# Layer 3 attention: how the mixed bank is turned, summed over its halves and divided

## The chip, the cores and the metric

The kernel runs on one core of a Trainium2 chip. The metric is device time in microseconds (us) of one launch, which computes a whole four-layer decoder. The engines are TensorE (PE, with its weight loads as PEld), VectorE (DVE), ScalarE (ACT), GpSimd (POOL) and the DMA queues. They run side by side and meet at semaphores.

## The reference

Each of the four layers has self-attention, cross-attention and a feed-forward part; `x` is 16 x 128 x 256, 2048 tokens of 256 features. The change touches only the attention of layer 3, which lets all 2048 tokens attend to each other, in 16 heads of 16 features:

```python
proj = jnp.einsum('bsd,ed->bse', x, proj_w) + proj_b
flat = jnp.transpose(proj.reshape(B, S, H, hd), (2, 0, 1, 3)).reshape(H, B * S, hd)
q = jnp.einsum('hnd,hde->hne', flat, wq)
k = jnp.einsum('hnd,hde->hne', flat, wk)
logits = jnp.einsum('hne,hme->hnm', q, k) / jnp.sqrt(jnp.asarray(D, x.dtype))
attn = jax.nn.softmax(logits, axis=-1)
out = jnp.einsum('hnm,hmd->hnd', attn, flat)
```

`out` is put back into token order and added to `x`.

## The kernel before

The kernel is a row of phases. In a phase every engine has its own program, written out in a fixed order, and waits on semaphores by count; a phase ends when all its engines have ended. The phase here is called "heads" (`l3_attn`, second half). It takes the 16 heads as 8 pairs and the 2048 queries as 4 chunks of 512, which makes 32 units `u` of 32 steps `n`. A step handles one tile of 128 keys of one of the pair's two heads (`a`).

All engines count the same steps:

- PE, `probe` (L4821): computes logits the other way round (queries on partitions), 48 steps ahead, only to find each query's maximum. They go through four banks of PSUM, two for each pair of steps.
- DVE, `peak_of` (L4874): the maximum over two such banks. After a unit's 16 of these, `peak_of_all` (L4880) reduces once more, and POOL and DVE (`part`, `turn_rows`, `lay_rows`) put the maximum into two extra rows of the queries.
- PE, `score` (L4811): keys on partitions, 512 queries along the row, less the maximum. Three banks (`SB`) take turns. ACT, `exp` (L4911), reads the bank and writes `attn`.
- PE, `mix` (L4836): values times `attn`, some eight steps behind. A bank holds four strips of 32 partitions: two heads times two halves of the key tiles. Row 16 of a strip is the softmax's sum, since the values carry a column of ones (`VW` is 17 of `PAD` 32).

When a unit's mixing is done, its end is worked off in the following unit, at fixed steps:

- step 6: ACT copies the mixed bank to `output` in SBUF (`out`, L4922). The next `mix` waits for it.
- step 15: PE turns `output` with four 128 x 128 transposes (`unturn`, L4846) into the next of the three score banks; the slot counts as one of the "score" jobs.
- step 15: ACT copies the whole turned bank to `unturned` (`take`, L4928), which frees the bank: `slot_free` waits on the common counter `read`, which `exp` and `take` raise.
- step 17: POOL adds the two halves (`add_halves`, L4984) to `sums`.
- step 24: DVE takes the reciprocal of the softmax's sums (L4891); POOL multiplies (L4990) and adds the product to `x` (L4994).

Between steps 14 and 16 PE has no probe and score to run beside each other until the turning is over: score 15 stands in front of it, and the probes of step 16 behind it.

Of the kernel before, what the change touches and what calls it, by code (L numbers as in the profile page):

```python
# [13 lines left out]
ALU = mybir.AluOpType  # L14
ACT = mybir.ActivationFunctionType
# [17 lines left out]
def sl(i, n=P):  # L33
    return slice(i * n, (i + 1) * n)
# [4479 lines left out]
def l3_attn(k):  # L4514
# [23 lines left out]
    with ExitStack() as stack:  # L4538
# [185 lines left out]
        peak = sb(k, stack, "peak", [P, 2, 4, 2])  # L4724
        peak_parts, peak_rows = (sb(k, stack, m, [P, 2, 4, 2, PAD]) for m in ("peak_parts", "peak_rows"))
        output = sb(k, stack, "output", [P, CHUNK])
        unturned = sb(k, stack, "unturned", [P, 4, 4, PAD])
        sums, fresh = sb(k, stack, "sums", [P, 4, 2, VW]), sb(k, stack, "fresh", [P, 4, 2, D])
        share = sb(k, stack, "share", [P, 4, 2])
        mixed_bank = k.ps[:, 7, :]  # L4730
        steps = range(-LEAD, TOTAL + SPAN)
        OUT, UNTURN, SUM, DIVIDE, TURN, RAISE = 6, 15, 17, 24, 5, 8

        def scored(n):
            return 0 <= n < TOTAL
# [10 lines left out]
        for n_ in steps:  # L4746
# [3 lines left out]
            for job in jobs:  # L4750
                slot_of[job] = len(slot_of)

        def bank(job):
            return k.ps[:, slot_of[job] % SB, :]

        names = ("loaded0 loaded1 pool_step cleared fetched probed maxed peaked parted rows_turned raised scored read mixed outed "
                 "unturned summed shared added value_made value_took biased")
        with phase(k, "heads", names) as (block, s):
            loaded = [s[f"loaded{i}"] for i in range(2)]

# [25 lines left out]
            @block.tensor  # L4786
            def _(pe):
                def slot_free(job):
                    if slot_of[job] >= SB:
                        pe.wait_ge(s["read"], slot_of[job] - SB + 1)  # L4790
                    else:
                        pe.wait_ge(s["value_took"], QT // 2)

                def value(t):
                    i, o = t // 2, t % 2
                    if i >= SB and o == 0:
                        pe.wait_ge(s["value_took"], i - SB + 1)
                    for kt in range(KD):
                        last = nc.tensor.matmul(k.ps[:, i % SB, sl(o, DIM)], xT[t // GROUP][:, kt, sl(t % GROUP)], wp[:, kt, :],
                                                start=kt == 0, stop=kt == KD - 1)  # L4800
                    if o:
                        last.then_inc(s["value_made"], 1)

                def score(n):
                    u, i = n // SPAN, n % SPAN
                    pair, c, kt, a = u // CHUNKS, u % CHUNKS, i // 2, i % 2
                    rows = slice(TILE * a, TILE * a + DEEP)
                    if i == 0:
                        pe.wait_ge(s["raised"], 8 * (u + 1))
                    slot_free(("score", n))  # L4810
                    nc.tensor.matmul(bank(("score", n)), keys[pair % 2][rows, sl(kt)], queries[pair % 2][rows, sl(c, CHUNK)],  # L4811
                                     start=True, stop=True).then_inc(s["scored"], 1)

                def probe(p):
                    pair, t, c, a = p // (CHUNKS * SPAN), p // 8 % QT, p // 2 % 4, p % 2
                    rows = slice(TILE * a, TILE * a + DEEP)
                    if p % (CHUNKS * SPAN) == 0:
                        pair_landed(pe, pair)
                    if p >= PB and p % 2 == 0:
                        pe.wait_ge(s["maxed"], (p - PB) // 2 + 1)  # L4820
                    last = nc.tensor.matmul(k.ps[:, SB + p % PB, :], queries[pair % 2][rows, sl(t)], keys[pair % 2][rows, sl(c, CHUNK)],  # L4821
                                            start=True, stop=True)
                    if p % 2:
                        last.then_inc(s["probed"], 1)

                def mix(m, half):
                    u, part = m // 8, m % 8
                    columns = sl(half, CHUNK // 2)
                    if half == 0:
                        pe.wait_ge(s["read"], slot_of["score", 4 * m + 3] + 1)  # L4830
                    if part == 0 and half == 0:
                        pe.wait_ge(s["fetched"], u // CHUNKS + 1)
                        if u >= 1:
                            pe.wait_ge(s["outed"], u)
                    for strip in range(4):
                        last = nc.tensor.matmul(mixed_bank[sl(strip, PAD), columns], head_values[:, u // CHUNKS % 2, strip % 2, 2 * part + strip // 2, :],  # L4836
                                                attn[:, (4 * m + strip) % RING, columns], start=part == 0 and half == 0, stop=part == 7 and half == 1,
                                                skip_group_check=True)
                    if half == 1:
                        last.then_inc(s["mixed"], 1)  # L4840

                def unturn(u):
                    pe.wait_ge(s["outed"], u + 1)
                    slot_free(("unturn", u))
                    for b in range(4):
                        last = nc.tensor.transpose(bank(("unturn", u))[:, sl(b)], output[:, sl(b)], k.ident[:, :])  # L4846
                    last.then_inc(s["unturned"], 1)

                for n in steps:
                    if n % 2 == 0:  # L4850
                        for p in (n + LEAD, n + LEAD + 1):
                            if p < TOTAL:
                                probe(p)
                        if 0 <= (n + LEAD) // 2 - 1 < QT:
                            value((n + LEAD) // 2 - 1)
                        if scored(n):
                            score(n)
                        if scored(4 * (n // 4 - 2)):
                            mix(n // 4 - 2, n % 4 // 2)
                        if scored(n + 1):  # L4860
                            score(n + 1)
                    if ended_at(n, UNTURN) is not None:
                        unturn(ended_at(n, UNTURN))

            @block.vector
            def _(dve):
# [20 lines left out]
                                peak_parts[:, r % 2, :, :, :].rearrange("p b a c -> p (b a c)")).then_inc(s["rows_turned"], 1)  # L4887

                def divide(u):
                    dve.wait_ge(s["summed"], u + 1)  # L4890
                    v.reciprocal(share[:, :, :].unsqueeze(3), sums[:, :, :, D:VW]).then_inc(s["shared"], 1)  # L4891

                for n in steps:
                    p = n + LEAD
                    if p < TOTAL:
# [10 lines left out]
            def _(act):  # L4906
# [11 lines left out]
                def out(u):  # L4918
                    act.wait_ge(s["mixed"], 8 * (u + 1))
                    if u >= 1:  # L4920
                        act.wait_ge(s["unturned"], u)
                    nc.scalar.activation(output[:, :], mixed_bank, ACT.Copy).then_inc(s["outed"], 1)  # L4922

                def take(u):
                    act.wait_ge(s["unturned"], u + 1)
                    if u >= 1:
                        act.wait_ge(s["summed"], u)
                    nc.scalar.activation(unturned[:, :, :, :].rearrange("p b a w -> p (b a w)"), bank(("unturn", u)),  # L4928
                                         ACT.Copy).then_inc(s["read"], 1)

                for i in range(QT // 2):
                    take_values(i)
                for n in steps:
                    if scored(n):
                        exp(n)
                    if ended_at(n, OUT) is not None:
                        out(ended_at(n, OUT))
                    if ended_at(n, UNTURN) is not None:
                        take(ended_at(n, UNTURN))

            @block.gpsimd
            def _(pool):
# [43 lines left out]

                def add(u):
                    pair, c = u // CHUNKS, u % CHUNKS
                    pool.wait_ge(s["shared"], u + 1)
                    g_.tensor_tensor(fresh[:, :, :, :], sums[:, :, :, 0:D], share[:, :, :].unsqueeze(3).broadcast_to([P, 4, 2, D]),  # L4990
                                     ALU.mult).then_inc(s["added"], 1)
                    pool.wait_ge(s["added"], 2 * u + 1)
                    x = k.x[:, sl(c, 4), sl(pair, 2 * D)].rearrange("p b (a d) -> p b a d", a=2)
                    g_.tensor_tensor(x, x, fresh[:, :, :, :], ALU.add).then_inc(s["added"], 1)  # L4994
                    done["added"] += 2

                def add_bias(i):
                    pool.wait_ge(s["value_took"], i + 1)
# [8 lines left out]
                for n in steps:  # L5007
# [8 lines left out]
                        lay_rows(row_at(n, RAISE))  # L5016
                    if n > 0 and n % (CHUNKS * SPAN) == CHUNKS * SPAN - 16 and n // (CHUNKS * SPAN) + 1 < PAIRS:
                        fetch(n // (CHUNKS * SPAN) + 1)
                    if ended_at(n, SUM) is not None:
                        add_halves(ended_at(n, SUM))  # L5020
                    if ended_at(n, DIVIDE) is not None:
                        add(ended_at(n, DIVIDE))


def lay_out_rest(i, w):
# [224 lines left out]
```

## Time and profile before

| | |
|---|---|
| Time, median of 3 runs | 3270.43 us (3260.84 to 3272.57) |
| The profiled execution's own time | 3283.28 us |
| Its span | 3281.5 us |
| Granted TensorE clock, mean over the span | 0.951 |
| The phase "heads" | about 2300 to 3030 us of the span |
| Units in it | 32 |

A row of the timeline merges instructions of one kind that follow each other: its count is behind the x, and its length reaches from the first one's start to the last one's end. An f32 matmul appears as two records (and two weight loads); a transpose and an fp32r matmul (probe, score) as one. Matmuls are pipelined and their ends are modelled, so the starts are what a reader should compare.

### The profile page before, as it was taken

The page shows a single profiled execution, that of the slowest core. Times are in us where ns is not written, and L with a number is a line of the kernel's source. Part 1 is how long each engine was busy: PE and PEld are TensorE (multiplying, and loading weights), DVE is VectorE, ACT ScalarE, POOL GpSimd, SP SyncE. Part 2 cuts the span into 40 slices and gives each one's busy share as a digit, 9 for nine tenths or more (in the row PEclk, how much of TensorE's full clock was granted, in tenths as well). Part 3 has the DMA queues.
Part 4 walks back from the last instruction along what each step waited for, and adds up shares of the span by engine and source line. Part 5 has one row for each costly group of instructions (what it writes and reads, how often), then busy time and mean ns, then how long its engine had stood idle before and what let it go on. Part 6 is the DMA issues. An engine that isn't in the chain of part 4 may idle for free. (4 is left out here: it accounts for less than half of the span.)

```text
span 3281.5 us, 59482 instructions
## 1 busy us (share of the span) xinstructions
PE 2987.2 (91%) x20953; PEld 1853.7 (56%) x20957; DVE 2145.8 (65%) x4263; ACT 1900.2 (58%) x4408; POOL 1131.2 (34%) x1285
## 2 busy tenths in 40 slices
PE   7979889999988899988799989898899999999989
PEld 4656568888755466634577656454333333333667
DVE  6767663233586566676677557425699999995672
ACT  7958725555443344445666635212388888888554
POOL 4535555442450122223366643101222211211333
PEclk9989879999999999999899999899699999999989
DMA  9400056676640000031000051223311111100300
GB/s 310 138 10 1 1 231 201 211 216 182 189 128 2 26 1 1 1 131 62 5 1 1 1 193 53 91 87 119 77 21 21 21 21 21 21 2 20 124 1 26
DMA packets 158996, 243.69 MB, mean 74 GB/s; under 512 B 21450, under 2 KB 130666, under 8 KB 153434
## 3 DMA queue, kind: packets, MB, share of 16 engines
q1 hardware_dynamic: 144690, 201.93, 19.9%
q0 software_dynamic: 13824, 37.77, 3.6%
q8 instruction: 173, 2.83, 0.4%
q14 instruction: 117, 0.96, 0.1%
q10 hardware_dynamic: 192, 0.20, 0.0%
HBM read 131.14 MB, written 107.12 MB: 73 GB/s over the span
## 5 line engine op out<-in xcount | busy, mean ns | idle before, releaser
L4874 DVE TENSOR_REDUCE peaks<-ps 128x2 f32<-128x1024 f32 x512 | 619.0, 1220 | 63.1 <-PE ps L4821 61.2
L4911 ACT ACTIVATE attn<-ps 128x512 f32<-128x512 f32 x1024 | 558.9, 596 | 99.4 <-PE ps L4811 42.2
L4821 PE MATMUL ps<-keys,queries 50*128 50x512 f32 x1024 | 367.6, 463 | 19.0 <-DMA queries<-parts 15.4
L4811 PE MATMUL ps<-queries,keys 50*128 50x512 f32 x1024 | 383.4, 454 | 0.0
L4836 PE MATMUL ps<-attn,head_values 128*32 128x256 f32 x4096 | 331.8, 396 | 9.2 <-ACT output L4922 9.2
L4811 PEld LDWEIGHTS ps<-queries,keys 50*128 50x128 f32 x1024 | 157.3, 188 | 215.2 <-ACT attn L4911 197.1
L1239 POOL TENSOR_TENSOR attn_w<-attn_w,attn_share 128x512 f32<-128x512 f32 x128 | 131.7, 1050 | 373.8 <-DVE attn_share L1085 373.8
L2163 PE MATMUL ps<-experts,tileT 128*128 x884 | 227.9, 379 | 2.0 <-ACT tileT L2242 2.0
L2413 DVE COPY hiddenT<-ps 128x128 f32<-128x128 f32 x237 | 69.0, 291 | 245.1 <-PE ps L2170 242.7
L4836 PEld LDWEIGHTS ps<-attn,head_values 128*32 128x32 f32 x4096 | 82.3, 108 | 197.7 <-issue 108.1
L4821 PEld LDWEIGHTS ps<-keys,queries 50*128 50x128 f32 x1024 | 146.4, 189 | 34.1 <-issue 26.1
L2163 PEld LDWEIGHTS ps<-experts,tileT 128*128 128x128 f32 x884 | 150.7, 190 | 17.2 <-issue 2.3
L2248 ACT ACTIVATE gate<-ps 128x128 f32<-128x128 f32 x237 | 65.8, 278 | 161.3 <-PE ps L2163 159.2
L2183 PE MATMUL ps<-experts,hiddenT 128*128 (+1 forms) x474 | 144.6, 387 | 7.3 <-issue 3.5
L1076 DVE TENSOR_REDUCE attn_peak<-ps 128x4 f32<-128x512 f32 x128 | 87.6, 685 | 95.5 <-PE ps L958 95.5
L4961 POOL CAST peak_parts<-peak 128x8 fp32r<-128x8 f32 x32 | 6.3, 197 | 399.8 <-DVE peak L4880 381.1
L2075 POOL DMA_INDIRECT rows<-expert_rows,index x96 | 94.0, 979 | 110.9 <-ACT normed L2259 71.6
L972 PE MATMUL ps<-xT,L_xattn_Wq 128*128 128x512 f32 x256 | 124.7, 610 | 7.7 <-ACT qT L1176 6.2
L2062 POOL DMA_INDIRECT routed_rows<-rows,index x96 | 96.8, 1009 | 83.5 <-ACT normed L2259 47.8
L4976 POOL CAST queries<-peak_rows 2x128 fp32r<-2x128 f32 x256 | 73.5, 287 | 123.5 <-DVE peak_rows L4886 109.8
L4334 POOL TENSOR_TENSOR lasting<-lasting,pairs 128x512 f32<-128x512 f32 x64 | 81.0, 1279 | 85.3 <-ACT lasting L4259 85.3
L1187 ACT ACTIVATE attn_wT<-ps 128x512 f32<-128x512 f32 x128 | 70.5, 594 | 67.5 <-PE ps L989 67.5
(732 smaller groups left out, 7189.8 us busy)
## 6 DMA issues: line engine op xcount, KB each, us to landing
tile_in<-routed_rows SPq DMA_DIRECT2D x244, 128.0 KB, 2.3
expert_rows<-normed SPq DMA_DIRECT2D x136, 128.0 KB, 1.9
routed_rows<-zeros SPq DMA_DIRECT2D x2, 8064.0 KB, 48.2
experts<-in_L_ffn_experts SPq DMA_DIRECT2D x4, 3072.0 KB, 20.8
routed_rows<-zeros SPq DMA_DIRECT2D x1, 12160.0 KB, 66.0
expert_rows<-is_it SPq DMA_DIRECT2D x85, 128.0 KB, 2.2
kT<-L_xattn_keys SPq DMA_DIRECT2D x8, 1024.0 KB, 4.9
v<-L_xattn_values SPq DMA_DIRECT2D x8, 1024.0 KB, 8.4
```

Source lines behind the costliest of these rows:

```text
L972: last = nc.tensor.matmul(query_bank, wq[:, kt, sl(4 * p + jj)], xT[g % 2][:, kt, :], start=kt == 0, stop=kt == KD - 1)
L1076: link(v_.tensor_reduce(peak[:, n % 2, side, :], scores(side), AX.X, ALU.max))
L1239: nc.gpsimd.tensor_tensor(w, w, share[:, n % 2, side, :].unsqueeze(2).broadcast_to([P, 4, P]), ALU.mult).then_inc(s_["scaled"], 1)
L2062: nc.gpsimd.indirect_dma_start(rows_dram[g][:, :], bass.IndirectOffsetOnAxis(index_of(slice(t, t + 1))[:, 0, c:c + 1], 0), rows[:, t, :], ...
L2075: nc.gpsimd.indirect_dma_start(rows[:, TOP * (t % 2) + c, :], None, back_dram[g][:, :], bass.IndirectOffsetOnAxis(index[:, t, c:c + 1], 0) ...
L2163: last = nc.tensor.matmul(gate_bank(u), x, weight(u, 2 * kt * INNER, 2 * INNER), start=False, stop=kt == KD - 1)
L2183: nc.tensor.matmul(out_bank(u), hiddenT[:, u % 2, :], weight(u, 2 * KD * INNER, DIM), start=is_tile(u), stop=True).then_inc(s["downed"], 1)
L4811: nc.tensor.matmul(bank(("score", n)), keys[pair % 2][rows, sl(kt)], queries[pair % 2][rows, sl(c, CHUNK)], start=True, stop=True).then_in ...
L4821: last = nc.tensor.matmul(k.ps[:, SB + p % PB, :], queries[pair % 2][rows, sl(t)], keys[pair % 2][rows, sl(c, CHUNK)], start=True, stop=True)
L4836: last = nc.tensor.matmul(mixed_bank[sl(strip, PAD), columns], head_values[:, u // CHUNKS % 2, strip % 2, 2 * part + strip // 2, :], attn[ ...
L4874: v.tensor_reduce(peaks[:, r % 2, i // CHUNKS, :, i % CHUNKS], k.ps[:, at:at + 2, :], AX.X, ALU.max).then_inc(s["maxed"], 1)
L4911: nc.scalar.activation(attn[:, n % RING, :], bank(("score", n)), ACT.Exp, scale=1.0 / 16.0).then_inc(s["read"], 1)
```

## The change

`unturn` no longer transposes. It multiplies `output` by `fold`, a 128 x 34 matrix of zeros and ones that VectorE builds once at the phase's start, as a sum of strips of the identity. Its product is the turned bank with the two halves already added: 34 columns for each of the four token tiles. ACT's `take` and POOL's `add_halves` are gone, with the tiles `unturned` and `sums`. VectorE's `divide`, moved from step 24 to step 16, waits for the product, takes the reciprocal out of PSUM and multiplies out of PSUM into `fresh`; that frees the bank (semaphore `divided`). POOL only adds `fresh` to `x`. Since `read` now counts exponentials alone, `slot_free` asks which kind of job had the bank before.

```diff
@@ slot_free
-                        pe.wait_ge(s["read"], slot_of[job] - SB + 1)
+                        kind, at = jobs_in_order[slot_of[job] - SB]
+                        pe.wait_ge(s["read" if kind == "score" else "divided"], at + 1)
@@ unturn
+                    if u == 0:
+                        pe.wait_ge(s["folding"], 1)
                     for b in range(4):
-                        last = nc.tensor.transpose(bank(("unturn", u))[:, sl(b)], output[:, sl(b)], k.ident[:, :])
-                    last.then_inc(s["unturned"], 1)
+                        last = nc.tensor.matmul(bank(("unturn", u))[:, sl(b, 2 * VW)], output[:, sl(b)], fold[:, :, :].rearrange("p a v -> p (a v)"),
+                                                start=True, stop=True)
+                    last.then_inc(s["folded"], 1)
@@ VectorE
                 def divide(u):
-                    dve.wait_ge(s["summed"], u + 1)
-                    v.reciprocal(share[:, :, :].unsqueeze(3), sums[:, :, :, D:VW]).then_inc(s["shared"], 1)
+                    dve.wait_ge(s["folded"], u + 1)
+                    if u >= 1:
+                        dve.wait_ge(s["added"], u)
+                    both = bank(("unturn", u))[:, 0:8 * VW].rearrange("p (b a v) -> p b a v", b=4, a=2)
+                    v.reciprocal(share[:, :, :].unsqueeze(3), both[:, :, :, D:VW]).then_inc(s["shared"], 1)
+                    dve.wait_ge(s["shared"], u + 1)
+                    v.tensor_tensor(fresh[:, :, :, :], both[:, :, :, 0:D], share[:, :, :].unsqueeze(3).broadcast_to([P, 4, 2, D]),
+                                    ALU.mult).then_inc(s["divided"], 1)
+                strips = k.ident[:, :].rearrange("p (s a c) -> p s a c", s=2, a=2)
+                v.tensor_tensor(fold[:, :, :], strips[:, 0, :, 0:VW], strips[:, 1, :, 0:VW], ALU.add).then_inc(s["folding"], 1)
@@ ScalarE: take
-                    nc.scalar.activation(unturned[:, :, :, :].rearrange("p b a w -> p (b a w)"), bank(("unturn", u)),
-                                         ACT.Copy).then_inc(s["read"], 1)
@@ GpSimd: add_halves, add
-                    g_.tensor_tensor(sums[:, :, :, :], unturned[:, :, 0:2, 0:VW], unturned[:, :, 2:4, 0:VW], ALU.add).then_inc(s["summed"], 1)
-                    g_.tensor_tensor(fresh[:, :, :, :], sums[:, :, :, 0:D], share[:, :, :].unsqueeze(3).broadcast_to([P, 4, 2, D]),
-                                     ALU.mult).then_inc(s["added"], 1)
                     x = k.x[:, sl(c, 4), sl(pair, 2 * D)].rearrange("p b (a d) -> p b a d", a=2)
                     g_.tensor_tensor(x, x, fresh[:, :, :, :], ALU.add).then_inc(s["added"], 1)
```

On PE, at step 15 of a unit, this is what stood between score 15 and the next probes (`queries_323`, `keys_325` are the pair's operands, `keys_326` and `queries_324` those of the next pair):

```order
L4836 MATMUL ps<-attn,head_values 32x256 x4
L4811 MATMUL ps<-queries_323,keys_325 128x512
L4846 MATMUL ps<-ident,output 128x128 x4
L4821 MATMUL ps<-keys_326,queries_324 128x512 x2
L4811 MATMUL ps<-queries_323,keys_325 128x512
```

And this is what stands there in the changed kernel, where the same program lines are L4838, L4813 and L4823:

```order
L4838 MATMUL ps<-attn,head_values 32x256 x4
L4813 MATMUL ps<-queries_323,keys_325 128x512
L4850 MATMUL ps<-fold,output 128x34 x4
L4823 MATMUL ps<-keys_326,queries_324 128x512 x2
L4813 MATMUL ps<-queries_323,keys_325 128x512
```

Nothing moved on PE: four instructions were replaced by four others at the same place.

On VectorE, around a unit's last maximum (`peak`), the order before was:

```order
L4874 TENSOR_REDUCE peaks<-ps 128x2 x12
L4880 TENSOR_REDUCE peak<-peaks 128x8
L4874 TENSOR_REDUCE peaks<-ps 128x2 x3
L4886 STREAM_TRANSPOSE peak_rows<-peak_parts 128x256
L4874 TENSOR_REDUCE peaks<-ps 128x2
L4891 RECIPROCAL share<-sums 128x8
```

Now it is (maxima L4879 and L4885, the turning L4891):

```order
L4879 TENSOR_REDUCE peaks<-ps 128x2 x13
L4885 TENSOR_REDUCE peak<-peaks 128x8
L4899 RECIPROCAL share<-ps 128x8
L4901 TENSOR_TENSOR fresh<-ps,share 128x128
L4879 TENSOR_REDUCE peaks<-ps 128x2 x3
L4891 STREAM_TRANSPOSE peak_rows<-peak_parts 128x256
```

The reciprocal moved ahead of four maxima, to the place directly behind `peak`, and has the product behind it.

## Rows read from the trace of the kernel before

**Rows 1.** Windows view, a full stretch: length, busy us (count) by engine, clock, DMA.

```profile
2600.00:2700.00 100.00, 98.57 (x934) 37.30 (x929) 94.59 (x91) 87.69 (x163) 19.90 (x63) 1.00 0.22 31
```

**Rows 2.** Grouped lines, 2340 to 3035 us: busy us, mean ns, idle before and releaser.

```profile
L4911 ACT ACTIVATE attn<-ps 128x512 f32<-128x512 f32 x1024 | 558.9, 596 | 99.4 <-PE ps L4811 42.2
...
L4836 PE MATMUL ps<-attn,head_values 128*32 128x256 f32 x4096 | 331.8, 396 | 9.2 <-ACT output L4922 9.2
...
L4846 PE MATMUL ps<-ident,output 128*128 128x128 f32 x128 | 21.0, 286 | 0.7 <-ACT output L4922 0.7
...
L4928 ACT ACTIVATE unturned<-ps 128x512 f32<-128x512 f32 x32 | 19.1, 597 | 0.7 <-PE ps L4846 0.7
...
L4990 POOL TENSOR_TENSOR fresh<-sums,share 128x128 f32<-128x128 f32 x32 | 12.9, 402 | 3.0 <-DVE share L4891 0.6
```

**Rows 3.** Timeline within a unit: start us, length us, engine, line, operation, idle before.

```profile
2704.89 10.95 ACT L4911 ACTIVATE attn<-ps 128x512 f32<-128x512 f32 x18 [0.15 <-PE ps L4811]
...
2706.59 10.85 DVE L4874 TENSOR_REDUCE peaks<-ps 128x2 f32<-128x1024 f32 x9
...
2706.82 0.50 PE L4811 MATMUL ps<-queries,keys 50*128 50x512 f32 x1
...
2708.05 0.50 PE L4811 MATMUL ps<-queries,keys 50*128 50x512 f32 x1
```

**Rows 4.** Timeline of all engines where the bank is turned.

```profile
2699.65 0.49 PE L4811 MATMUL ps<-queries,keys 50*128 50x512 f32 x1
2700.07 0.42 PEld L4846 LDWEIGHTS ps<-ident,output 128*128 128x128 f32 x4 [0.24 <-issue]
...
2700.66 0.50 PE L4821 MATMUL ps<-keys,queries 50*128 50x512 f32 x2
...
2700.76 0.60 ACT L4928 ACTIVATE unturned<-ps 128x512 f32<-128x512 f32 x1
...
2701.00 0.39 PE L4811 MATMUL ps<-queries,keys 50*128 50x512 f32 x1
2701.27 1.23 DVE L4874 TENSOR_REDUCE peaks<-ps 128x2 f32<-128x1024 f32 x1 [0.64 <-PE ps L4821]
...
2701.43 0.60 ACT L4911 ACTIVATE attn<-ps 128x512 f32<-128x512 f32 x1
...
2701.89 0.49 PE L4811 MATMUL ps<-queries,keys 50*128 50x512 f32 x1
```

**Rows 5.** Timeline of ScalarE in the last unit, which has no probes.

```profile
2997.40 12.03 ACT L4911 ACTIVATE attn<-ps 128x512 f32<-128x512 f32 x22 [0.34 <-PE ps L4811]
```

**Rows 6.** Timeline, another stage: f32 matmuls of 32 moving columns and what follows.

```profile
500.22 0.63 PE L2103 MATMUL ps<-L_ffn_Wr,xT 128*128 128x32 f32 x4
500.78 0.40 PE L2101 MATMUL ps<-L_ffn_br,ones 1*128 1x32 f32 x2
```

**Rows 7.** Timeline, another stage: f32 matmuls of 8 moving columns, their loads.

```profile
2057.71 0.96 PE L2599 MATMUL ps<-L_ffn_Wg,xT 128*128 128x8 f32 x8
...
2057.61 0.97 PEld L2599 LDWEIGHTS ps<-L_ffn_Wg,xT 128*128 128x128 f32 x8
2058.60 0.30 PEld L1295 LDWEIGHTS ps<-L_xattn_Wv,ctxT 64*128 64x128 f32 x4
```

**Rows 8.** Windows view of those two places, columns as in rows 1.

```profile
500.20:501.00 0.80, 0.80 (x7) 0.74 (x6) 0.00 (x0) 0.00 (x0) 0.00 (x0) 1.00 0.46 164
2057.60:2058.60 1.00, 1.00 (x11) 0.98 (x10) 0.00 (x0) 0.60 (x1) 0.00 (x0) 1.00 0.00 0
```

**Rows 9.** Grouped lines of VectorE, whole span: a product read out of PSUM.

```profile
L2419 DVE TENSOR_TENSOR hidden<-ps,gate 128x128 f32<-128x128 f32 x237 | 66.7, 281 | 5.5 <-ACT gate L2248 5.0 <-issue 0.2
```

**Rows 10.** Timeline of the stage's end: last turning and last reciprocal.

```profile
3026.45 0.66 PE L4846 MATMUL ps<-ident,output 128*128 128x128 f32 x4 [0.72 <-ACT output L4922]
...
3028.33 0.20 DVE L4891 RECIPROCAL share<-sums 128x8 f32<-128x8 f32 x1 [11.99 <-POOL sums L4984]
```

More of the change, by code:

```diff
@@ L4726, in l3_attn @@
         output = sb(k, stack, "output", [P, CHUNK])
-        unturned = sb(k, stack, "unturned", [P, 4, 4, PAD])
-        sums, fresh = sb(k, stack, "sums", [P, 4, 2, VW]), sb(k, stack, "fresh", [P, 4, 2, D])
-        share = sb(k, stack, "share", [P, 4, 2])
+        fold = sb(k, stack, "fold", [P, 2, VW])
+        fresh, share = sb(k, stack, "fresh", [P, 4, 2, D]), sb(k, stack, "share", [P, 4, 2])
         mixed_bank = k.ps[:, 7, :]
         steps = range(-LEAD, TOTAL + SPAN)
-        OUT, UNTURN, SUM, DIVIDE, TURN, RAISE = 6, 15, 17, 24, 5, 8
+        OUT, UNTURN, DIVIDE, ADD, TURN, RAISE = 6, 15, 16, 24, 5, 8
         def scored(n):
@@ L4751, in l3_attn @@
                 slot_of[job] = len(slot_of)
+        jobs_in_order = sorted(slot_of, key=slot_of.get)
         def bank(job):
@@ L4756, in l3_attn @@
         names = ("loaded0 loaded1 pool_step cleared fetched probed maxed peaked parted rows_turned raised scored read mixed outed "
-                 "unturned summed shared added value_made value_took biased")
+                 "folding folded shared divided added value_made value_took biased")
         with phase(k, "heads", names) as (block, s):
@@ L4829, in mix @@
                     if half == 0:
-                        pe.wait_ge(s["read"], slot_of["score", 4 * m + 3] + 1)
+                        pe.wait_ge(s["read"], 4 * m + 4)
                     if part == 0 and half == 0:
@@ L4920, in out @@
                     if u >= 1:
-                        act.wait_ge(s["unturned"], u)
+                        act.wait_ge(s["folded"], u)
                     nc.scalar.activation(output[:, :], mixed_bank, ACT.Copy).then_inc(s["outed"], 1)
[L4924 to L4927, printed above, removed]
-                    nc.scalar.activation(unturned[:, :, :, :].rearrange("p b a w -> p (b a w)"), bank(("unturn", u)),
-                                         ACT.Copy).then_inc(s["read"], 1)
                 for i in range(QT // 2):
@@ L4937, in _ @@
                         out(ended_at(n, OUT))
-                    if ended_at(n, UNTURN) is not None:
-                        take(ended_at(n, UNTURN))
             @block.gpsimd
@@ L4988, in add @@
                     pair, c = u // CHUNKS, u % CHUNKS
-                    pool.wait_ge(s["shared"], u + 1)
-                    g_.tensor_tensor(fresh[:, :, :, :], sums[:, :, :, 0:D], share[:, :, :].unsqueeze(3).broadcast_to([P, 4, 2, D]),
-                                     ALU.mult).then_inc(s["added"], 1)
-                    pool.wait_ge(s["added"], 2 * u + 1)
+                    pool.wait_ge(s["divided"], u + 1)
                     x = k.x[:, sl(c, 4), sl(pair, 2 * D)].rearrange("p b (a d) -> p b a d", a=2)
                     g_.tensor_tensor(x, x, fresh[:, :, :, :], ALU.add).then_inc(s["added"], 1)
-                    done["added"] += 2
+                    done["added"] += 1
                 def add_bias(i):
@@ L5018, in _ @@
                         fetch(n // (CHUNKS * SPAN) + 1)
[L5019 to L5022, printed above, removed]
+                    if ended_at(n, ADD) is not None:
+                        add(ended_at(n, ADD))
 def lay_out_rest(i, w):
```

## The prediction

> **What bounds the kernel now.** I read the windows view first, to see which engine is full in this phase. In a stretch of 100 us PE is busy 98.57 us, VectorE 94.59, ScalarE 87.69 and GpSimd 19.90, at a granted clock of 1.00, which is the 2.4 GHz level [rows 1]. Three engines look nearly full, so the shares alone do not say who sets the pace; the timeline does. Inside a unit two steps take 2708.05 - 2706.82 = 1.23 us on PE [rows 3], and eleven such pairs in a row, from 2701.89 on, repeat that figure. Over the same time ScalarE does 18 exponentials in 10.95 us, 1.22 for two, and VectorE nine maxima in 10.85 us, 1.21 for each pair of steps [rows 3]: both are a little faster than PE and end up waiting for it. ScalarE could go much faster: in the last unit, where no probes stand between the scores, 22 exponentials take 12.03 us, 1.09 for two [rows 5]. Its idle time before the exponentials, 99.4 us, has the scores as its largest named releaser [rows 2]. PE's matmuls, on the other hand, show hardly any wait: 9.2 us before the mixing, where the bank is still being copied out, and 0.7 us before the turning [rows 2]. So PE sets the pace by the work it has, and VectorE and ScalarE follow with slack.
>
> Then the place that the change touches. Between two first scores around the turning there are 2701.89 - 2699.65 = 2.24 us instead of 1.23 [rows 4, 3]: 1.01 us extra in each unit. It has two parts, which follow one another on PE. Score 15 has no probe to run beside, and 0.42 us go by until the first weight load of the turning at 2700.07; from there to the next probes at 2700.66 are 0.59 us [rows 4]. PE makes up none of it, since the pace after it is 1.23 again.
>
> **The change, part by part.**
>
> *ScalarE's copy goes* (32 times 0.60 us by its grouped line [rows 2]). It ran from 2700.76 to 2701.36. The next exponential started at 2701.43, but its score ended only at 2701.00 + 0.39 = 2701.39 [rows 4]: the copy lay entirely beside PE's late probes and score. Gain on the path: nothing. What was late behind it, PE, is late still.
>
> *GpSimd's sum and product go.* GpSimd is busy a fifth of the stretch [rows 1], and nobody waits for these two except the reciprocal and the addition, which end in mid-unit. Gain: nothing, except at the stage's very end (below).
>
> *VectorE's reciprocal moves and gets a product.* VectorE waits 0.64 us before the maximum at 2701.27 for the delayed probes [rows 4]. The reciprocal (0.20 at the end of the stage [rows 10]) and the product go into that hole. A product of the same shape out of PSUM takes 281 ns [rows 9]. With what is worked out for PE below, the turned bank is ready about 1.06 us after its first load (2057.71 + 0.96 - 2057.61 [rows 7]), thus at 2701.13. VectorE started 0.11 us after the end of the matmuls that it waited for (2700.66 + 0.50 against 2701.27 [rows 4]). So reciprocal 2701.24 to 2701.44, product, allowing 0.05 for the wait between, to about 2701.77. The probes behind the turning, moved by the same amount as PE, would let the maximum start at 2701.27 + 0.41 = 2701.68. VectorE is late by some 0.1 us, once a unit, and makes that up at 1.21 against 1.23 within a few pairs. The four probe banks leave PE two pairs ahead, so PE sees nothing of it; the turned bank is wanted back by the third score after it, which comes after 2701.89 + 0.41 = 2702.30. Cost: nothing. If the cover were gone, each 0.1 us of it would cost 31 times 0.1, 3 us.
>
> *The fold's own making*, one small product on VectorE before the first probe has arrived: nothing.
>
> *PE: four transposes become four f32 matmuls.* This is the term that counts. Each of the new ones is two records, each with a weight load of 128 columns, because the data in `output` is the stationary side and changes every time. The trace has two such streams in other stages, both at a granted clock of 1.00 [rows 8]. Four records of 32 moving columns, from the first start to the next instruction's: 500.78 - 500.22 = 0.56 us [rows 6]. Eight records of 8 moving columns, from the first load to the load of the next, narrower matmul: 2058.60 - 2057.61 = 0.99 us [rows 7]. By the eight loads in 0.97 us a record costs 0.11 to 0.12, and that is what binds: 8 columns or 32 make no visible difference. Extending the four records by four more gives 0.56 + 4 x 0.11 = 1.00. I take 1.00 against 0.59 for the transposes, so PE is later by 0.41 us in a unit. 31 of the 32 turnings stand between scores: 31 x 0.41 = 12.7 us.
> Bounds for it, from the same rows: below, the fold could be no dearer than the transposes (0), if the loads hid behind score 15; above, without any overlap between two groups of four, 2 x 0.56 - 0.59 = 0.53, or 16.4 us.
>
> One rule of the Trainium skill speaks against the change. "Perfetto Trace Analysis", section "Transposes", advises using the transpose operation for a logical transposition and not an ordinary matmul, as there is special logic to skip the arithmetic; the trace agrees so far as a transpose comes as one record and an f32 matmul as two. The rule has no figure; the sign by it is the one forecast, whatever the columns.
>
> *The end of the stage.* The last unit's end has nothing beside it, so there the shorter chain counts. Before, from the end of the turning at 3026.45 + 0.66 = 3027.11 to the reciprocal at 3028.33 are 1.22 us of copy and sum [rows 10]; of these 0.11 remain as the wait's latency, so 1.11 go. The product costs 0.28 in place of 0.40 [rows 9, 2], so 0.12 more go, and the fold takes 0.41 more. Together -0.8 us.
>
> **Sum.** 12.7 - 0.8 = +11.9 us. The profiled execution took 3283.28 us, and would take 3295.2. It lies 12.85 us above the median of the three runs, so on the median I forecast 3270.43 + 11.9 = 3282.3 us, 0.36% slower.
>
> **Rivals.**
>
> *The columns decide, not the loads.* Moving columns hardly change: four transposes of 128, 512 in all, against four products of 34, which are 544 if each of the two records streams its columns twice. If PE hid the loads, the turning would take what it takes now, and only the stage's end is left: 3270.43 - 0.8 = 3269.6. For it: 0.24 us of idle before the first load, in which a load could go ahead [rows 4]. Against it: the eight records of 8 columns, which take the same 0.99 us that this rule would put at far less [rows 7]. Chance 0.12. The skill's "TensorE: Matmul & The Clock Gate", section "Back-to-back issue gap", has a table of this kind: 134 cycles at 128 columns and about 60 at 64 or fewer, by which eight records would be an estimated 0.20 us and four transposes 0.22. The rows do not follow it where each matmul has a new stationary side.
>
> *ScalarE's relief reaches the path* (the other side). If the pace at the turning was set by ScalarE, taking the copy out would give back 0.60 us in each of 32 units, -19.2 us, 3251.2. For it: 87.69 us busy in 100 [rows 1], and the copy sits right before the delayed exponential. It decides if that exponential's score is ready before the copy ends. It is not, by 0.03 us [rows 4], and the gain would need PE to be no slower as well. Chance 0.07.
>
> *VectorE becomes the late one.* Reciprocal and product stand in front of three maxima and of the turning of the rows. If together they take over 0.5 us more than I allow, the third score waits for the bank, and the probes for the maxima. An overrun of 0.8 us would cost 0.3 us in 31 units, 9.3 us more: 3291.6. For it: VectorE is 94.59 us busy [rows 1]. Against it: the product's row has exactly this shape and source [rows 9]. Chance 0.11.
>
> **How the numbers follow.** The forecast, 0.30 to 0.53 us in a unit, has 0.70. Its own range is 31 x 0.30 - 0.8 to 31 x 0.53 - 0.8, +8.5 to +15.6: 3278.9 to 3286.0. The runs shown lie 11.7 us apart, so a median of the changed kernel may lie a few us to either side. The 80% range takes in the columns' rival at its lower end and VectorE's at its upper: 3268 to 3293. A measurement of this kernel tells 0.5%, 16.4 us, from no change; the limits are 3254.1 and 3286.8. Faster: 0.07, ScalarE's rival. Slower by over 0.5%: 0.12 of the forecast's 0.70 (its upper end, or runs that measure it high), most of VectorE's 0.11, and 0.04 for the fold's switch costing more: 0.26. Within: 0.67.
>
> **What would show it.** In the changed profile the first score before the turning and the first after it should be 2.65 us apart instead of 2.24, with 1.00 between the fold's first load and the next probe's; the pace inside a unit stays 1.23. ScalarE's idle time grows by what its copy took. The reciprocal and the product fill VectorE's hole, and the maximum behind them waits little or not for PE. I am wrong if the fold's eight records take 0.7 us or less, if the pace inside a unit changes, or if scores wait for the product.

## The result, and the profile after

The changed kernel takes 3283.66 us (median of 20 runs, 3271.36 to 3292.54) against 3271.11 for the kernel before (20 runs, 3255.44 to 3285.30). The ratio is 1.0037, with a 95% interval of 1.0026 to 1.0048: slower by 8.5 to 15.7 us. The forecast was 11.9 us.

Single executions of one kernel lie up to 30 us apart, so the profiled executions must not be compared by their spans. The changed kernel's span was 3269.5 us, 12 us shorter than the one before, though the kernel is slower. Its phase began 11.8 us earlier (first maximum of the phase at 2296.30 instead of 2308.13), and in the phase's first part the granted clock stood at 0.50 for 17.10 us instead of 34.10. The windows views of these two stretches (length, busy time by engine, clock, DMA), first the kernel before:

```profile
2338.90:2373.00 34.10, 32.67 (x165) 12.09 (x165) 24.08 (x23) 16.87 (x31) 5.10 (x17) 0.50 0.00 0
```

and the changed one:

```profile
2327.60:2344.70 17.10, 16.20 (x79) 6.63 (x77) 13.21 (x13) 9.28 (x17) 1.27 (x4) 0.50 0.00 0
```

What the change did is read from the place that repeats. The copies of the mixed bank mark the units. Two of them in the middle of the phase, in the kernel before:

```profile
2610.29 0.60 ACT L4922 ACTIVATE output<-ps 128x512 f32<-128x512 f32 x1
2631.38 0.60 ACT L4922 ACTIVATE output<-ps 128x512 f32<-128x512 f32 x1
```

and in the changed one:

```profile
2616.80 0.60 ACT L4935 ACTIVATE output<-ps 128x512 f32<-128x512 f32 x1
2638.31 0.60 ACT L4935 ACTIVATE output<-ps 128x512 f32<-128x512 f32 x1
```

A unit took 21.09 us and takes 21.51, which is 0.42 to 0.43 more. From the first copy of the phase to the last, 31 units that contain 31 turnings, are 660.68 us (2358.64 to 3019.32) where there were 647.46 (2378.34 to 3025.80): 13.2 us more. The timeline of a turning in the changed kernel answers to [rows 4]:

```profile
2707.87 0.49 PE L4813 MATMUL ps<-queries,keys 50*128 50x512 f32 x1
2708.29 0.97 PEld L4850 LDWEIGHTS ps<-fold,output 128*128 128x128 f32 x8 [0.24 <-issue]
2708.29 1.08 PE L4850 MATMUL ps<-fold,output 128*128 128x34 f32 x8
...
2709.30 0.50 PE L4823 MATMUL ps<-keys,queries 50*128 50x512 f32 x2
2709.41 0.21 DVE L4899 RECIPROCAL share<-ps 128x8 f32<-128x8 f32 x1 [0.56 <-PE ps L4850]
...
2709.65 0.29 DVE L4901 TENSOR_TENSOR fresh<-ps,share 128x128 f32<-128x128 f32 x1
2709.91 1.23 DVE L4879 TENSOR_REDUCE peaks<-ps 128x2 f32<-128x1024 f32 x1
2710.06 0.60 ACT L4924 ACTIVATE attn<-ps 128x512 f32<-128x512 f32 x1 [1.07 <-PE ps L4813]
2710.53 0.50 PE L4813 MATMUL ps<-queries,keys 50*128 50x512 f32 x1
...
2711.76 0.50 PE L4813 MATMUL ps<-queries,keys 50*128 50x512 f32 x1
```

The reader is to see four things. From the first load to the next probe are now 1.01 us, where there were 0.59. The 0.42 us ahead of the first load (2707.87 to 2708.29) are what they were, so that the two first scores around the turning are 2.66 us apart instead of 2.24. The pace behind it is 1.23 again. And ScalarE, which has no copy there any more, simply waits 1.07 us for the score. The grouped lines (busy us, mean ns, idle before) from the first copy of the mixed bank to the last, first of the kernel before, then of the changed one, show ScalarE's part for all these units:

```profile
L4911 ACT ACTIVATE attn<-ps 128x512 f32<-128x512 f32 x986 | 538.3, 596 | 79.1 <-PE ps L4811 22.5
```

```profile
L4924 ACT ACTIVATE attn<-ps 128x512 f32<-128x512 f32 x986 | 538.2, 596 | 110.4 <-PE ps L4813 53.5
```

ScalarE's idle time before the exponentials grew by 31.3 us. That is the 18.5 us of the 31 copies that are gone and the 13.2 us by which PE takes longer: all of the copies' time was turned into waiting. PE's fold, over the whole phase, is 256 records, eight for each of the 32 turnings, with hardly a wait:

```profile
L4850 PE MATMUL ps<-fold,output 128*128 128x34 f32 x256 | 34.6, 280 | 0.7 <-ACT output L4935 0.7
```

At the phase's end, from the last copy of the mixed bank to the next phase's first table load, the kernel before took 4.06 us:

```profile
3025.80 0.60 ACT L4922 ACTIVATE output<-ps 128x512 f32<-128x512 f32 x1 [1.30 <-PE ps L4836]
...
3029.86 1.28 ACT L1162 ACT_TABLE_LOAD   x1 [2.12 <-PEq L61]
```

and the changed one 3.16, with one reciprocal, one product and one addition behind the fold:

```profile
3019.32 0.60 ACT L4935 ACTIVATE output<-ps 128x512 f32<-128x512 f32 x1 [1.30 <-PE ps L4838]
...
3021.09 0.21 DVE L4899 RECIPROCAL share<-ps 128x8 f32<-128x8 f32 x1 [12.09 <-PE ps L4850]
...
3022.48 1.28 ACT L1162 ACT_TABLE_LOAD   x1 [2.56 <-PEq L61]
```

That gives back 0.9 us: 13.2 - 0.9 = 12.3, against 12.1 by the ratio and 12.55 between the two medians.

### The profile page after: what moved, and what is told of

Its sections match the earlier page's. It is cut to its first block and busy times, and to the rows that moved or that the text cites. A ratio compares the mean times of both kernels' runs of the same rounds, so it can differ in the third digit from the quotient of the medians.

```text
span 3269.5 us, 59647 instructions
## 1 busy us (share of the span) xinstructions
PE 2974.0 (91%) x21085; PEld 1854.9 (57%) x21085; DVE 2159.2 (66%) x4296; ACT 1881.5 (58%) x4376; POOL 1104.0 (34%) x1221
## 5 line engine op out<-in xcount | busy, mean ns | idle before, releaser
L4879 DVE TENSOR_REDUCE peaks<-ps 128x2 f32<-128x1024 f32 x512 | 619.4, 1222 | 27.8 <-PE ps L4823 25.8
L4823 PE MATMUL ps<-keys,queries 50*128 50x512 f32 x1024 | 363.4, 457 | 18.9 <-DMA queries<-parts 14.8
L4813 PE MATMUL ps<-queries,keys 50*128 50x512 f32 x1024 | 380.2, 451 | 0.0
L4838 PE MATMUL ps<-attn,head_values 128*32 128x256 f32 x4096 | 328.7, 393 | 9.2 <-ACT output L4935 9.2
L4813 PEld LDWEIGHTS ps<-queries,keys 50*128 50x128 f32 x1024 | 155.9, 186 | 212.1 <-ACT attn L4924 194.2
L4838 PEld LDWEIGHTS ps<-attn,head_values 128*32 128x32 f32 x4096 | 82.0, 108 | 195.8 <-issue 105.0
L4823 PEld LDWEIGHTS ps<-keys,queries 50*128 50x128 f32 x1024 | 144.6, 187 | 29.7 <-issue 20.9
```

The lines of the kernel that those rows point to most:

```text
L4879: v.tensor_reduce(peaks[:, r % 2, i // CHUNKS, :, i % CHUNKS], k.ps[:, at:at + 2, :], AX.X, ALU.max).then_inc(s["maxed"], 1)
```

## The experiments

The theory was that the whole loss is PE's time for the fold, set by its eight weight loads. The rivals were the moving columns, and VectorE's new chain in front of the maxima. "Unit" is the distance of two copies of the mixed bank in the middle of the phase, as above; the ratio is to runs of the kernel before taken beside each experiment, with its 95% interval. Three kernels ran once only and are judged by their units alone; the phase's middle is at a granted clock of 1.00 in all but the run with six products more.

| Kernel | unit, us | ratio |
|---|---|---|
| before | 21.09 | 1 |
| changed | 21.51 | 1.0037 [1.0026, 1.0048] |
| transposes, halves added by VectorE | 21.09, each fourth 21.11 | 0.9986 [0.9973, 0.9999] |
| fold in fp32r | 21.05 | 0.9989 [0.9974, 1.0005] |
| fold of 128 columns | 21.59 | one run, 3291.84 us |
| fold before score 15 | 21.09 | 0.9991 [0.9974, 1.0008] |
| one product more | 21.51 | one run, 3288.71 us |
| six products more | 22.08, six units longer | one run, 3359.50 us |
| transposes, moved | 20.72, each fourth 21.11 | 0.9972 [0.9956, 0.9988] |
| fold in fp32r, moved | 20.63 | 0.9946 [0.9926, 0.9965] |
| kernel before, turning moved | 20.67 | 0.9967 [0.9948, 0.9987] |

**Transposes back, the rest of the change kept.**

```diff
-                        last = nc.tensor.matmul(bank(("unturn", u))[:, sl(b, 2 * VW)], output[:, sl(b)], fold[:, :, :].rearrange("p a v -> p (a v)"),
-                                                start=True, stop=True)
+                        last = nc.tensor.transpose(bank(("unturn", u))[:, sl(b)], output[:, sl(b)], k.ident[:, :])
...
+                    both = bank(("unturn", u)).rearrange("p (b s a w) -> p b a w s", b=4, s=2, a=2)
+                    v.tensor_reduce(sums[:, :, :, :], both[:, :, :, 0:VW, :], AX.X, ALU.add).then_inc(s["folding"], 1)
+                    dve.wait_ge(s["folding"], u + 1)
```

> The changed kernel with the four transposes put back on PE in place of the fold; VectorE adds the halves out of PSUM by a small reduction, then takes the reciprocal and the product, all at step 16, and ScalarE's copy stays out. Load theory (the whole loss is PE's time for the fold, 0.43 us a unit; all else is hidden): copies of the mixed bank 21.09 us apart as in the kernel before, and a time 0 to 1 us under it. Rival (VectorE's chain in front of the maxima, or the wait for it, costs): units still at 21.4 or more, since VectorE's chain is here longer by some 0.4 us than in the changed kernel, and a time 9 us or more above the kernel before.

The unit is 21.09 us, the loss is gone. VectorE's chain is longer here than in the changed kernel, by the addition of 0.44 us, as the timeline shows (the bank is turned at about 2699.68):

```profile
2699.71 0.44 DVE L4896 TENSOR_REDUCE sums<-ps 128x136 f32<-128x272 f32 x1
2700.19 0.20 DVE L4898 RECIPROCAL share<-sums 128x8 f32<-128x8 f32 x1
2700.43 0.29 DVE L4900 TENSOR_TENSOR fresh<-sums,share 128x128 f32<-128x128 f32 x1
2700.64 1.22 DVE L4876 TENSOR_REDUCE peaks<-ps 128x2 f32<-128x1024 f32 x1
```

So VectorE's chain costs nothing in its new place, and taking out ScalarE's copy gains nothing where PE does the same work: with the copy and without it a unit is 21.09. The time is under the kernel before by 4.6 us according to the ratio; its interval, 0.3 to 8.8 us, holds the upper end of the 0 to 1 us expected.

**One record instead of two.**

```diff
-        output = sb(k, stack, "output", [P, CHUNK])
-        fold = sb(k, stack, "fold", [P, 2, VW])
+        output = sb(k, stack, "output", [P, CHUNK], F32R)
+        fold = sb(k, stack, "fold", [P, 2, VW], F32R)
```

> The changed kernel with the output copy and the fold matrix in the type fp32r, so that each of the fold's four matmuls is one record with one load instead of two; the sums are rounded a little more by it. Load theory: 0.56 to 0.60 us from the first load to the next probe instead of 1.01, units 21.07 to 21.11 us, time 0 to 1 us under the kernel before. Rival (a matmul with data as its stationary side costs more than a transpose whatever the number of records, or VectorE's chain costs): units at 21.3 or more.

The loads of the fold, and the next probes:

```profile
2689.86 0.52 PEld L4850 LDWEIGHTS ps<-fold,output 128*128 128x128 f32 x4 [0.24 <-issue]
...
2690.41 0.50 PE L4823 MATMUL ps<-keys,queries 50*128 50x512 f32 x2
```

0.55 us instead of 1.01: four loads fewer, 0.46 less, and the unit falls by the same 0.46 to 21.05. That is 0.02 under the expected span. A fold with data as its stationary side is here no dearer than a transpose (0.59 us), so long as it has one load for each tile.

**The same loads, more columns.**

```diff
-        fold = sb(k, stack, "fold", [P, 2, VW])
+        fold = sb(k, stack, "fold", [P, 4, PAD])
...
-                        last = nc.tensor.matmul(bank(("unturn", u))[:, sl(b, 2 * VW)], output[:, sl(b)], fold[:, :, :].rearrange("p a v -> p (a v)"),
+                        last = nc.tensor.matmul(bank(("unturn", u))[:, sl(b)], output[:, sl(b)], fold[:, :, :].rearrange("p a v -> p (a v)"),
```

> The changed kernel with a fold of 128 columns (34 in use, the others not read) instead of 34: the same eight loads, 3.8 times the moving columns. Load theory: a record of 256 columns of the mixing follows the one before it after 0.24 us, so one of 128 columns needs about 0.12, hardly over the 0.112 of a load; units 21.55 to 21.70 us. Columns theory (moving columns set the fold's price): the fold's records grow with the columns, 1.0 us to over 2 us, units 22.5 us or more.

```profile
2704.11 0.97 PEld L4850 LDWEIGHTS ps<-fold,output 128*128 128x128 f32 x8 [0.24 <-issue]
2705.20 0.19 PEld L4823 LDWEIGHTS ps<-keys,queries 50*128 50x128 f32 x2
```

With 3.8 times the columns the eight loads take the same 0.97 us, and from the first to the next probe's load are 1.09 us instead of 1.01. The unit is 21.59 us. The columns' rival falls: up to 128 columns the stream of eight records costs its loads, and 0.08 us more at its end.

The last two experiments change the number of records and the columns that each record moves, never the length of a load. A price of the record itself, whatever its load, was therefore not tested. Rows of another stage of the changed kernel, also at a granted clock of 1.00, speak against it. There 64 f32 records with loads of 32 columns and 64 moving columns take 1.03 us from the first load to the next instruction's, 0.016 us each:

```profile
945.93 0.94 PEld L3335 LDWEIGHTS ps<-near_k,values 128*32 128x32 f32 x64 [0.76 <-issue]
946.96 0.30 PEld L3326 LDWEIGHTS ps<-L_attn_W_v,xT 128*128 128x128 f32 x2
```

Each of them uses only 32 of the array's columns, and the fold's records all 128, so several may be under way side by side: the rows show that a record can be had for far less than 0.11 us, and not by themselves that the length of its load makes the difference.

**The fold before score 15.**

```diff
+                        if ended_at(n + 1, UNTURN) is not None:
+                            unturn(ended_at(n + 1, UNTURN))
                         if scored(n + 1):
                             score(n + 1)
-                    if ended_at(n, UNTURN) is not None:
-                        unturn(ended_at(n, UNTURN))
```

(The slots of the three score banks are numbered in the same new order.)

> The changed kernel with the fold issued before score 15 instead of behind it: it then follows the mixing, which also uses all rows of the array, and score 15 runs beside the next probe again. If the 0.42 us between score 15 and the first load of the turning are a lone score's time, they go, with a part of the switch: units about 21.0 to 21.1 us, time about that of the kernel before, 12 us under the changed one. Rival (those 0.42 us are a wait of the turning for the copy of the mixed bank or the slot, and move along with it): units stay at 21.5.

```profile
2694.81 0.64 PE L4838 MATMUL ps<-attn,head_values 128*32 128x256 f32 x8
2695.38 1.08 PE L4850 MATMUL ps<-fold,output 128*128 128x34 f32 x8
2696.39 0.49 PE L4813 MATMUL ps<-queries,keys 50*128 50x512 f32 x1
2696.39 0.72 PE L4823 MATMUL ps<-keys,queries 50*128 50x512 f32 x2
```

The fold takes its 1.01 us here too, but score 15 and the next probes now start together, at 2696.39. The unit is 21.09 us, 0.42 under the changed kernel: the time of a lone score, which stood in the kernel before as well. The step from the mixing to the fold is no shorter than one to a score: 0.57 us from the mixing's start to the fold's here (2694.81 to 2695.38), and 0.57 to a score's in the kernel before (2699.08 to 2699.65).

**VectorE's margin.** One, and then six, products more in each unit, whose results nothing uses; the edit for six (`range(1)` for one):

```diff
+                    for _ in range(6):
+                        v.tensor_tensor(spare[:, _, :, :, :], both[:, :, :, 0:D], share[:, :, :].unsqueeze(3).broadcast_to([P, 4, 2, D]), ALU.mult)
                     v.tensor_tensor(fresh[:, :, :, :], both[:, :, :, 0:D], share[:, :, :].unsqueeze(3).broadcast_to([P, 4, 2, D]),
                                     ALU.mult).then_inc(s["divided"], 1)
```

> The changed kernel with one product more on VectorE in each unit, between the reciprocal and the product that counts; its result is not read. It makes VectorE's chain behind the fold some 0.2 us longer. Theory (VectorE's chain has a margin of about 0.67 us, from the product's end to the load of the third score behind the fold): units stay 21.51 us. Rival (the chain is on the path): units 21.7 us, 6 us in all.

> The changed kernel with six such products more in each unit. They make VectorE's chain some 1.2 to 1.3 us longer, 0.5 to 0.6 beyond the margin of 0.67. Theory: the third score behind the fold now waits for the bank, units 22.0 to 22.2 us. Rival (VectorE runs beside PE without any such limit, or catches up through the probe banks): 21.51. Rival (the chain is on the path from its start): 22.7.

With one more the unit stays 21.51 us. With six more it is 22.08, and PE's load of the third score waits for the product:

```profile
2700.33 1.28 DVE L4903 TENSOR_TENSOR spare<-ps,share 128x128 f32<-128x128 f32 x6
...
2701.53 0.28 DVE L4904 TENSOR_TENSOR fresh<-ps,share 128x128 f32<-128x128 f32 x1
...
2701.86 0.18 PEld L4814 LDWEIGHTS ps<-queries,keys 50*128 50x128 f32 x1 [0.36 <-DVE fresh L4904]
```

So the wait that the prediction's third rival named is there, it decides only beyond the margin, and the changed kernel is clear of it. The whole run took 3359.50 us, more than 31 times 0.57 explains. Six units are longer than 22.08 (27.81, 31.67 and 23.72 us, twice), 34 us in all, since the granted clock fell in them, as told at the end; and the first copy of the phase came at 2389.54 instead of 2358.64.

**The transposes, moved; the fp32r fold, moved.** Both of the edits above joined, for each kind of turning.

> Both steps that helped by themselves: four transposes, halves added by VectorE, and the turning issued before score 15. If the two gains are of different things (fewer loads; a score that runs beside a probe) they add: units 21.51 - 0.42 - 0.42 = 20.67 us, time 13 to 14 us under the kernel before, ratio 0.9955 to 0.9965. If the moved turning's loads already ran beside other work, less than half of that.

> The fold in fp32r (one record each, sums rounded a little more) and issued before score 15: units 21.05 - 0.42 = 20.63 us, time 14 to 15 us under the kernel before, ratio 0.995 to 0.996. If the gains don't add: units 20.9 us or more.

The fp32r fold's unit is the expected one, 20.63 us. Its ratio, 0.9946, is just under the expected 0.995 to 0.996: some 17.7 us under the kernel before, with an interval of 11.5 to 24.2 that holds the 14 to 15 expected. The gains of the two edits add. The transposes fall short: 20.72 us, each fourth unit 21.11, ratio 0.9972. PE no longer sets the pace alone there. VectorE is at 97.64 us of 100:

```profile
2600.00:2700.00 100.00, 98.86 (x946) 37.66 (x944) 97.64 (x102) 85.31 (x159) 16.53 (x56) 1.00 0.18 25
```

and in each fourth unit, where GpSimd copies the next pair's values, VectorE's product takes 0.67 us instead of 0.29:

```profile
2583.64 0.67 DVE L4900 TENSOR_TENSOR fresh<-sums,share 128x128 f32<-128x128 f32 x1
...
2604.74 0.29 DVE L4900 TENSOR_TENSOR fresh<-sums,share 128x128 f32<-128x128 f32 x1
```

```profile
2583.51 0.67 POOL L4953 COPY head_values<-values 128x544 f32<-128x544 f32 x1
```

The probes that follow in this unit start 0.42 us behind their score (2585.08) instead of 0.03 as in the next unit, and their load waits for VectorE's maximum:

```profile
2585.08 0.49 PE L4813 MATMUL ps<-queries,keys 50*128 50x512 f32 x1
2585.50 0.19 PEld L4823 LDWEIGHTS ps<-keys,queries 50*128 50x128 f32 x2 [0.23 <-DVE peaks L4876]
```

That a product delayed by 0.38 us leads to a unit 0.39 us longer is read from these rows; it was not tested by moving the copy. Why the other units are 20.72 and not the expected 20.67 was not tested either.

**The kernel before, its turning moved.** The same edit of PE's order as above, and in ScalarE's program `take` ahead of that step's exponential.

> The kernel before with one edit: its turning is issued before score 15 instead of behind it (and ScalarE's copy before that step's exponential). ScalarE's copy, GpSimd's sum and product stay. If the 0.42 us of the lone score are independent of the fold, units go from 21.09 to 20.67 us and the time falls by about 13 us, ratio 0.995 to 0.997. If ScalarE's copy, which now stands in front of an exponential, reaches the path, units are 20.8 us or more.

```profile
2608.00 0.66 PE L4846 MATMUL ps<-ident,output 128*128 128x128 f32 x4
2608.58 0.50 PE L4811 MATMUL ps<-queries,keys 50*128 50x512 f32 x1
2608.59 0.73 PE L4821 MATMUL ps<-keys,queries 50*128 50x512 f32 x2
```

20.67 us, ratio 0.9967, some 10.8 us under the kernel before (4.3 to 17.1; 13 were expected): the lone score's 0.42 us have nothing to do with the change, and ScalarE's copy stays hidden even in front of an exponential.

## Why the prediction was right

- **What bounds the kernel.** PE, by its own work. Shown from both sides: ScalarE's copy out of a unit leaves it at 21.09, and 0.21 us more on VectorE leaves it at 21.51, while four records and their loads fewer on PE take 0.46 off and a lone score less takes 0.42 off.
- **The term that counts.** The fold was put at 1.00 us against 0.59; it is 1.01. The 12.7 us for 31 turnings became 13.2. The 1.00 came from two streams of f32 matmuls in other stages [rows 6, 7], and their loads behaved here as there.
- **VectorE's chain.** The turned bank was expected to be worked on from 1.17 us behind the first load, and the product to end at 1.70. It is 1.12 and 1.65. The maximum behind it started 0.61 us after the probes' start, the same as in the kernel before (2709.30 to 2709.91, 2700.66 to 2701.27): the 0.1 us by which the chain was expected to be late are not there.
- **ScalarE, GpSimd.** Nothing gained, as forecast. The prediction's grounds were 0.03 us between the copy's end and the score's; the better ground is that the copy could be taken away in a kernel with the same PE work, and nothing moved. Its idle time grew by more than the copy's time, since PE's delay came on top.
- **The phase's end.** -0.8 us forecast, -0.9 measured.
- **The rivals.** The columns' rival is excluded by the wide fold, ScalarE's by the transposes put back. VectorE's exists, but its margin was put at over 0.5 us, and by the run with six products it is about 0.63: they add 1.20 us, and 0.57 came through.
- **The rule on transposes** ("Perfetto Trace Analysis", "Transposes", of the Trainium skill) had the right sign, but the runs here do not show its ground: what made the ordinary matmul dear were its two records for f32 data. In fp32r it is level with the transpose (0.55 us against 0.59).

The sum was close because its largest term was; the forecast that the profiled execution would take 3295.2 us was not borne out (3271.36), since single executions differ by more than the change. One thing was in plain sight and not asked: 0.42 us ahead of the first load stand in the prediction as a given, and without giving up f32 they were the one gain over the kernel before that the units show.

## What to carry to other kernels

Where PE sets the pace, a matmul that takes over the work of other engines must be priced by its weight loads: with new data on its stationary side an f32 matmul cost two loads here, 0.11 us each, with 8 moving columns as with 128. Work taken off engines that follow gained nothing before the phase's end. And look at what an odd instruction does to its neighbours: the turning uses all 128 rows of the array, a score and a probe 50 each. Put between a score and the probes it split a pair that runs together, at 0.42 us; put next to the mixing, which also uses 128 rows, it did not.

## What was not expected of the hardware

- Up to 128 moving columns a stream of f32 records goes at the pace of its loads: with 8, 34 or 128 columns, eight loads of 128 columns took 0.97 us each time.
- A VectorE product of two operands in SBUF took 0.67 us instead of 0.29 while GpSimd copied 128 x 544 elements in SBUF; it ended 0.13 us after the copy (2584.31 against 2584.18). With the transposes put back and not moved, where the product started later in the copy, it took 0.45 us and again ended 0.13 us after it (2574.31 against 2574.18); the units of 21.11 us there are those with this copy:

```profile
2573.51 0.67 POOL L4953 COPY head_values<-values 128x544 f32<-128x544 f32 x1
```

```profile
2573.86 0.45 DVE L4900 TENSOR_TENSOR fresh<-sums,share 128x128 f32<-128x128 f32 x1
```

The changed kernel's product, which reads PSUM, took 291 to 293 ns in all 32 units, also where the same copy ran beside it (copy from 2580.26, product from 2580.57).

- In the run with six products more the granted clock fell from 2.4 to 1.2 GHz in the middle of the phase, for 13.70 and 27.30 us, and again for the same lengths 348.20 us later:

```profile
2486.60:2500.30 13.70, 13.70 (x81) 4.39 (x80) 8.89 (x9) 7.13 (x14) 2.75 (x9) 0.50 0.00 1
2500.30:2558.30 58.00, 57.14 (x524) 23.30 (x520) 54.58 (x71) 46.51 (x87) 7.33 (x25) 1.00 0.20 29
2558.30:2585.60 27.30, 27.30 (x153) 8.64 (x153) 16.71 (x15) 14.56 (x27) 2.75 (x9) 0.50 0.00 1
```

PE waited 0.36 us for the product once in each unit at the full clock, so why it fell in some of them stays open.
